# Sigmoid as exp, ln, exp on ScalarE: a fused recurrent layer with a ternary gate on eight cores

## The reference

```
xn    = (x - mean) / sqrt(var + 1e-5)
B     = xn @ W2 + b2 ; C = xn @ W3 + b3          # 16 numbers each
delta = softplus(xn @ W1 + b1)
s     = xn * delta * sum_n(B * C)
xh    = xn @ H                                   # Hadamard, 1024 x 1024, scaled
sc    = max(|xh|, 1e-5) / 7
q     = clip(round(xh / sc), -8, 7) * sc
wq    = ternary(weight) * mean(|weight|) of its row
o     = q @ wq^T
out   = x + s * o * sigmoid(o)
```

## Time and profile before

| what | us |
|---|---|
| median of 2 runs | 519.12 (518.97 to 519.27) |
| the profiled execution, slowest core | 518.19 |
| span of its slowest core (core 4) | 516.4 |
| spans of cores 0 to 3 | 513.9, 513.9, 511.6, 511.1 |
| spans of cores 4 to 7 | 516.4, 516.0, 514.8, 516.1 |
| mean granted TensorE clock, all cores | 0.871 to 0.886 |

### The profile page before, as it was taken

One profiled execution on the slowest core, in us unless ns is written; L12 is line 12 of the kernel. 1 busy time (PEld: TensorE's weight loads), 2 busy tenths in 40 slices (PEclk: granted clock), 3 DMA queues, 4 the chain that ended last, 5 costly groups with the idle time before them and its releaser, 6 DMA issues.

```text
span 516.4 us, 6962 instructions; the slowest of 8 cores (511.1 to 516.4 us)
## 1 busy us (share of the span) xinstructions
PE 343.2 (66%) x1664; PEld 149.4 (29%) x1696; DVE 342.0 (66%) x600; ACT 349.5 (68%) x386; POOL 256.8 (50%) x183
## 2 busy tenths in 40 slices
PE   0004160797879797888979889796979797874300
PEld 0002130343333343333434334242424343431100
DVE  0508888344886878788787877868786875566240
ACT  0622233478988898898898988979888987775000
POOL 6000151011556565655556665656565657574654
PEclk9998575699897989999989989798979898999755
DMA  7993320434546554545655656554544334224111
GB/s 142 241 235 107 111 74 0 81 83 83 119 109 140 113 134 124 122 124 133 133 122 125 125 133 147 114 133 99 149 122 124 82 83 102 61 62 122 41 43 78
DMA packets 80971, 57.76 MB, mean 112 GB/s; under 512 B 70435, under 2 KB 70564, under 8 KB 80932
## 3 DMA queue, kind: packets, MB, share of 16 engines
q1 hardware_dynamic: 72916, 34.19, 32.8%
q0 software_dynamic: 8016, 23.14, 13.8%
HBM read 25.93 MB, written 16.78 MB: 83 GB/s over the span
## 4 chain that ended last, share of the span: by engine, by line
PE 30%; ACT 22%; DVE 21%; issue 12%; DMA 6%; POOL 5%; DVEq 1%; SPq 1%; ACTq 0%; POOLq 0%
PE psZ L264 5%; PE psZ L265 5%; PE psXH L310 5%; PE psO L285 5%; PE psO L286 4%; DVE o3s L33 4%; ACT L33 4%; ACT xnb L33 3%; ACT xqm L33 3%; PE psXH L308 3%; ACT esb L33 3%; DMA xb<-x 3%; ACT s L33 3%; DVE tbf L33 3%; DMA xnT<-xnb 3%
## 5 line engine op out<-in xcount | busy, mean ns | idle before, releaser
L33 POOL TENSOR_TENSOR t4b<-t3b,o3s 128x1024 f32<-128x1024 f32 x32 | 75.8, 2370 | 131.1 <-DVE t3b L33 131.1
L33 ACT ACT_TABLE_LOAD x58 | 74.4, 1283 | 43.2 <-DVE o3s L33 21.8
L264 PE MATMUL psZ<-W1c,xnT 128*128 128x512 bf16 x256 | 102.8, 402 | 0.5 <-DVE bcw L33 0.5
L285 PE MATMUL psO<-ternT,xqT 128*128 128x512 bf16 x255 | 97.9, 384 | 5.5 <-DMA xqT<-xqb 5.5
L265 PE MATMUL psZ<-W1c,xnT 128*128 128x512 bf16 x256 | 101.3, 396 | 0.0
L286 PE MATMUL psO<-ternT,xqT 128*128 128x512 bf16 x256 | 97.9, 382 | 2.8 <-DMA xqT<-xqb 2.8
L310 PE MATMUL psXH<-Hs,vT 128*128 128x512 bf16 x128 | 60.7, 474 | 45.9 <-ACT xqm L33 37.8
L33 POOL TENSOR_TENSOR ob<-xb,t4b 128x1024 f32<-128x1024 f32 x32 | 75.4, 2355 | 4.6
L33 POOL TENSOR_TENSOR uT<-xnT 128x512 bf16<-128x512 bf16 x32 | 37.2, 1162 | 37.6 <-DMA xnT<-xnb 36.7
L33 DVE COPY o3s<-psO 128x1024 f32<-128x1024 f32 x32 | 39.2, 1225 | 20.3 <-POOL ob L33 13.4
L33 ACT ACTIVATE esb<-psZ 128x1024 f32<-128x1024 f32 x32 | 32.8, 1024 | 28.2 <-PE psZ L267 26.1
(11 more groups left out here) (50 smaller groups left out, 492.4 us busy)
## 6 DMA issues: line engine op xcount, KB each, us to landing
xb<-x SPq DMA_DIRECT2D x32, 512.0 KB, 5.2
out<-ob POOLq DMA_DIRECT2D x32, 512.0 KB, 3.1
wfst<-wf POOLq DMA_DIRECT2D x8, 512.0 KB, 4.3
W1c<-w POOLq DMA_DIRECT2D x8, 256.0 KB, 17.9
Hs<-hpk SPq DMA_DIRECT2D x1, 512.0 KB
xnT<-xnb SPq DMA_TRANSPOSE x32, 3.1
xqT<-xqb SPq DMA_TRANSPOSE x32, 3.2
W23s<-w POOLq DMA_DIRECT2D x1, 64.0 KB, 3.9
```

What stands on the lines that cost most here:

```text
L33: inst = fn(*a, **kw)
L264: pe.matmul(psZ1[:, 0:512], lh, W1c[ic][:, 0:512], start=(ic == 0), stop=False)
L285: pe.matmul(ps[:, 0:512], lh, ternT[:, ic * DM:ic * DM + 512], start=(ic == 0), stop=(ic == KC - 1))
```

## The change

The sigmoid is no longer one activation. ScalarE computes e = exp(-sa * psO) into `esb`, l = ln(e + 1) into `l2` (a buffer that was there and unused), and exp(-l) into `s2`, which is 1 / (1 + exp(-sa * psO)). `esb` is now written twice in a step, by the softplus and by this. The signal `sSIG` moves to the third of the three. The factor with the minus sign is a new number per row, `nsa`, which VectorE makes by one more instruction between `sa` and `inv`; `nsa` has the four buffers that `sa` had, and `sa` has two. The eight weight buffers `W1c` become one tensor `W1s` of eight parts, with the same DMAs and the same matmuls on it.

```diff
--- before.py
+++ after.py
@@ -82,7 +82,7 @@
         S = lambda n, sh, dt: es.enter_context(nc.sbuf_tensor(n, sh, dt))
         SEM = lambda n: es.enter_context(nc.semaphore(n))
 
-        W1c = [S(f"W1c{i}", [128, DM], BF16) for i in range(KC)]
+        W1s = S("W1s", [128, KC * DM], BF16)
         Hs = S("Hs", [128, 4 * (DM // 2)], BF16)
         W23s = S("W23s", [128, KC * 32], BF16)
         ternT = S("ternT", [128, KC * DM], BF16)
@@ -124,7 +124,7 @@
         mk1 = lambda n: [S(f"{n}{i}", [128, 1], F32) for i in range(2)]
         sumsq = mk1("ssq"); xsum = mk1("xsm"); mean = mk1("mean"); var = mk1("var")
         mk4 = lambda n: [S(f"{n}{i}", [128, 1], F32) for i in range(4)]
-        rs = mk1("rs"); nmrs = mk1("nmrs"); sa = mk4("sa")
+        rs = mk1("rs"); nmrs = mk1("nmrs"); sa = mk1("sa"); nsa = mk4("nsa")
         inv = mk1("inv"); dot = mk1("dot"); cc = mk4("cc")
         mx = S("mx", [128, 1], F32); mxc = S("mxc", [128, 1], F32); mxh = S("mxh", [128, 1], F32)
         msq = S("msq", [128, 1], F32); lnv = S("lnv", [128, 1], F32)
@@ -199,7 +199,7 @@
             g.dma_start(out=b23s[:], in_=b23_hbm[:]).then_inc(sWG, 16)
 
             def w1_load(ic):
-                g.dma_start(out=W1c[ic][:],
+                g.dma_start(out=W1s[:, ic * DM:(ic + 1) * DM],
                             in_=w1_hbm[ic * 128:(ic + 1) * 128, :]).then_inc(sWG, 16)
             def wf_load(oc):
                 if oc >= 3:
@@ -261,8 +261,8 @@
                     xT = xnT[t % 3]
                     for ic in range(KC):
                         lh = xT[:, ic * 128:(ic + 1) * 128]
-                        pe.matmul(psZ1[:, 0:512], lh, W1c[ic][:, 0:512], start=(ic == 0), stop=False)
-                        pe.matmul(psZ1[:, 512:1024], lh, W1c[ic][:, 512:1024], start=(ic == 0), stop=False)
+                        pe.matmul(psZ1[:, 0:512], lh, W1s[:, ic * DM:ic * DM + 512], start=(ic == 0), stop=False)
+                        pe.matmul(psZ1[:, 512:1024], lh, W1s[:, ic * DM + 512:(ic + 1) * DM], start=(ic == 0), stop=False)
                     pe.matmul(psZ1[:, 0:512], onesbf[:], b1s[:, 0:512], start=False, stop=True)
                     pe.matmul(psZ1[:, 512:1024], onesbf[:], b1s[:, 512:1024], start=False, stop=True).then_inc(sPEZ, 1)
                 if c == 0:
@@ -355,8 +355,9 @@
                 w_ = c - 3
                 if 0 <= w_ < nt:
                     ac.wait_ge(sO3S, w_ + 1)
-                    ac.activation(s2[w_ % 3][:], psO3x[w_ % 2][:], AF.Sigmoid,
-                                  scale=sa[w_ % 4][:], _inc=(sSIG, w_ + 1))
+                    ac.activation(esb[:], psO3x[w_ % 2][:], AF.Exp, scale=nsa[w_ % 4][:])
+                    ac.activation(l2[:], esb[:], AF.Ln, bias=1.0)
+                    ac.activation(s2[w_ % 3][:], l2[:], AF.Exp, scale=-1.0, _inc=(sSIG, w_ + 1))
                 if c == 0:
                     prep_evac(range(0, 5))
                 if c == 1:
@@ -395,9 +396,10 @@
                     dv.wait_ge(sPEXH, u + 1)
                     dv.tensor_reduce(mx[:], psXH[:], AX.X, ALU.max, apply_absolute_value=True)
                     dv.tensor_single_scalar(mxc[:], mx[:], 1e-5, ALU.max)
-                    dv.tensor_single_scalar(sa[u % 4][:], mxc[:], 1.0 / 7.0, ALU.mult)
-                    dv.reciprocal(inv[u % 2][:], sa[u % 4][:])
-                    dv.tensor_tensor(cc[u % 4][:], dot[u % 2][:], sa[u % 4][:], ALU.mult, _inc=(sMX, u + 1))
+                    dv.tensor_single_scalar(sa[u % 2][:], mxc[:], 1.0 / 7.0, ALU.mult)
+                    dv.tensor_single_scalar(nsa[u % 4][:], sa[u % 2][:], -1.0, ALU.mult)
+                    dv.reciprocal(inv[u % 2][:], sa[u % 2][:])
+                    dv.tensor_tensor(cc[u % 4][:], dot[u % 2][:], sa[u % 2][:], ALU.mult, _inc=(sMX, u + 1))
                 v4 = c + 4
                 if 0 <= v4 < nt:
                     dv.wait_ge(sLDa[v4 % 11], 16 * (v4 // 11 + 1))
```

## The result

| | before | after |
|---|---|---|
| median us (lowest to highest, runs) | 519.38 (517.58 to 519.94, 10) | 513.37 (509.38 to 515.39, 11) |
| ratio after / before, 95% interval | | 0.9887 (0.9861 to 0.9913) |
| span of the slowest core in the profiled execution | 516.4 (core 4) | 510.4 (core 3) |
| `esb` of tile 4, us from the start, mean of the 8 cores | 125.6 | 124.8 |
| from there to `esb` of tile 28 (24 steps), mean | 299.1 | 295.2 |

The kernel became 1.1% faster, 6.0 us; the forecast was 513.5. By the 2% bound this is no change, by the interval it is one. In the profiles the middle gave 3.9 us, the start 0.8, the end 34.3 - 30.8 = 3.5 less the 2.4 that came back behind it.

A forecast was written before the change was run, and what follows sets the result against it. No engine is full; a two-step loop between ScalarE, TensorE and VectorE bounds it, over a second loop at 11.95 us. 518.19 - 3.6 - 0.7 - 1.3 = 512.6, plus 0.93 for the median: 513.5 us, range 505 to 520.

The forecast's parts named there:

- ScalarE's pass, 3.6 us from 0.28 a pass: First load or exp to `lnv`, 5.02 to 4.74 us; 13 passes on the chain save 3.6 us, bounds 0 and 7.8.
- that rival: Each table switch also costs a 1380 ns drain on ScalarE; 3.0 us saved a pass, kernel 505.2 us, chance 0.03.
- The clock, 1.3 us: TensorE's clock falls after idle time before psXH; one long dip shortens by half of 8.5 - 5.8 us, saving 1.3.
- the dips: Falls of TensorE's clock after idle time; a rival had 0.28 us stop most of them, 505.2 us, chance 0.10.
- `nsa`, 0: The added VectorE instruction, 0.26 us a step ahead of `cc`, is hidden as `cc` waits for `t4b`'s end; cost 0.
- The bound of 3.1 us: Cost of `nsa` if the cover by `cc` is gone: 0.26 us x 12 steps that VectorE sets.
- The end, 0.7 us: From step 29 on, without the second load before `esb`, half of one load is saved: 0.7 us, bounds 0 and 1.3.
- The psO buffer, 0: Freed 1.0 us later, TensorE's psO waits some 0.4 us, within its idle time for `esb`; cost 0, at most 2 us.
- `W1s`, 0: Weights as one tensor move no instruction; DMAs and matmuls are the same; cost 0.
- The floor of 11.95 us: Second loop without ScalarE: GpSimd's `t4b`, `ob`, store, `uT`, then VectorE's `prod`, `dot`, `o3s`; 11.95 us a step.
- 505 us: Low end of the range 505 to 520 us, which takes in 11.95 us a step.
- `cc` late, 531 us: Rival: `nsa` makes `cc` miss its place before GpSimd's `ob`, 1.5 us later in 12 steps; 531 us, chance 0.05.

The follow-up runs named there:

- the kernel with one exp: The kernel before with one exp where the sigmoid stands, leaving out the rest of the sigmoid; 500.09 us, ratio 0.9628.
- seventeen instructions: The changed kernel with `mxc` and `sa` made by one VectorE instruction, so 17 a step again as before; 511.62 us, ratio 0.9863.

## Why the prediction was right

The number was right to 0.1 us, which is partly luck: some of its terms were off and cancelled. By the profiles, as means of the cores, the middle gave 3.9 us where two terms had 4.9 together, the end 1.1 where the term was 0.7, and the start 0.8, which no term had. Profiles of kernels that do the same work differ by some 1.5 us in the middle (299.1 and 300.8 with `W1s` alone; 295.2 and 296.7 with the psO buffer freed early), so terms of this size can't be checked closely.

**ScalarE's pass, 3.6 us from 0.28 a pass.** The size of a pass was right to the hundredth (4.74 us), the loads were gone but one, and the activations took 1.11, 1.06 and 1.06 us. Two loads less were 2.57 us less, in the kernel with one exp, so no drain comes with a switch here. The Trainium skill, "ScalarE: Activation LUTs", section "What ACT_TABLE_LOAD costs", gives 1380 ns for one; the measurement decides, and that rival is out. How the pass reached the time is only partly as worked out. In the middle, 24 passes of 0.28 are 6.7 us, of which 3.9 became time and 2.2 more waiting of ScalarE. Nor did 13 passes each give 0.28: counted from `dot` to `dot`, a core had 8.0 steps of over 12.8 us before (13.5 on average) and 6.9 after (13.3), and 11.5 and then 15.6 of under 12.15. Most of the gain is steps that changed from a longer kind to the shortest, and fewer that became a little shorter.

**The clock, 1.3 us.** It can't be told apart. In the middle a core had 11.0 stretches at 1.2 GHz before and 11.2 after, so the dips didn't go; those longer than 5 us fell from 2.75 to 1.25, and the time at 1.2 GHz from 46.9 to 42.7 us. That is the direction of the term, and 4.3 us at half the clock would be at most 2.1 us of work, by my estimate. But with the psO buffer freed early, at the same time of the kernel, it was 47.4 us. TensorE's idle time before psXH didn't shrink (33.0 and 34.0 us), that before the small product did. The middle gave 3.9 us with `nsa` and 5.7 with seventeen instructions; how either divides between the shorter pass and shorter dips stays open.

**`nsa`, 0.** The cover was as described, `cc` had the same end. But the working looked only at the instruction's duration, and not at what it pushes: with it two `nmrs` a core were held for 1.5 us each. Added alone, it made the slowest core 2.2 us later by the medians and the mean of the cores 0.1, which is nothing; for the time of the kernel, which is that of the slowest core, the term was off, and its cause stays open. The bound of 3.1 us held, by luck, as it came from another mechanism.

**The end, 0.7 us.** Mis-sized. The stretch up to `esb` of tile 31 became 3.5 us shorter and 2.4 came back, as the last tiles go at GpSimd's pace; done alone it gave 0.2 us, nothing that can be measured.

**The start** wasn't in the sum: 0.8 us on average of the cores, in the first passes. No run isolates it; with one exp it was 3 us.

**The psO buffer, 0** and **`W1s`, 0** are shown by their experiments.

**The floor of 11.95 us** was the part that carried most. From `dot` to `dot` the first of the 24 steps took 11.1 us before and 10.8 after on every core, and none of the other 184 in either kernel was under 11.90. (From `esb` to `esb` single steps are shorter, 11.3 us from tile 27 to 28, since `esb` itself shifts within the step.) With one exp nearly all steps fell to it, the exceptions being the first ones. With one input of `prod` in PSUM it was gone. What I had wrong was what it leaves: 505 us was given as the least with it, and 500 was reached, by the start and by these first steps.

**`cc` late, 531 us.** The mechanism, the place and the edge were right: it decides between one and two more instructions. The price was too low, 37 us over the changed kernel instead of 18, since the miss comes in every step and not in 12.

## What to carry to other kernels

Before pricing a shorter pass on one engine, look for a second loop of about the same length that doesn't pass through that engine; here it was 11.95 us against 12.5, and it showed in a 16-number product that took 1.2 us. A small VectorE instruction with two tensors in SBUF beside a busy GpSimd is worth rewriting where something waits behind it: the one `prod` with an input from PSUM brought 9.6 us by the medians, more than the change studied here. All such rewrites and two merged pairs brought 12.8, of which what lies beyond `prod` is not clear step by step. An instruction added in a tight step must be priced by where it pushes the ones behind it, not by its own duration: a second one cost 3.6 us and a third 33.6.

## What the runs showed of the hardware

- A VectorE instruction of 128 x 1 with two tensors in SBUF was held as long as a GpSimd instruction ran (`cc` up to 2.35 us, `nmrs` 1.53), and with a scalar per row in place of the second tensor it was not (0.21 us). The Trainium skill, "SBUF — State Buffer", section "Who interferes with whom", says of two SBUF inputs that they contend with GpSimd's reads, and by that rule the traces agree; it says too that `tensor_scalar` can contend in its fast modes, and none of the 128 x 1 fp32 ones on the eight cores (`sa`, `nsa` and others) took more than 0.16 us in either kernel.
- Behind the issue of a store, the hold begins before GpSimd's instruction is shown: VectorE instructions that began 0.27 and 0.34 us ahead of `uT` were held until its end, one 0.36 us ahead on core 4 of the kernel after too (1.57 us), and not one 0.41 us ahead on core 3 of the kernel with seventeen instructions (0.18 us). Where `uT` had waited for a DMA, one 0.17 us ahead was not held.
- VectorE paused for 0.3 to 0.5 us between two of its own instructions, with no wait to explain it, at distances near 51 instructions and multiples of it: 102, 152, 51, 51, 51 and 49 on core 4 of the kernel before, 52, 102, 50, 104 and 51 on core 3 of the kernel after. With 17 instructions a step four of them in a row fell at the same place, with 18 they moved through the step, and in two steps one pushed `nmrs` into GpSimd's hold. The 51 is not the engine's own number. Counted with its semaphore instructions, which the timeline leaves out, the pauses of the kernel before stand ahead of instructions 59, 188, 315, 571, 955, 1084, 1213, 1342 and 1467, that is 128 or a multiple of it apart, within 3. This holds for all 926 such pauses (0.2 to 0.7 us) of the fourteen kernels and eight cores. So it is the place in VectorE's stream that decides, and every added instruction moves all the later ones against it. What the pause is, the runs don't show.
- A table switch cost 1.283 us and nothing beside it: the next activation began 0.01 us after each of the 464 loads of the eight cores of the kernel before, and a pass without its two loads was 2.57 us shorter.
